# Four gathers underway with a full wait at group ends, and float32r products ahead of the bucket product

## What is computed

```python
h = (x @ W.T).reshape(n, 8, 64)
e = leaky_relu(e_src[src] + e_dst[dst], 0.2) * (1.0 + et_emb[edge_type]) * edge_weight[:, None]
e = jnp.exp(e - e_max[dst])
alpha = e / (e_sum[dst] + 1e-10)
msg = h[src] * alpha[:, :, None]
out = jnp.zeros((n, 8, 64), x.dtype).at[dst].add(msg).reshape(n, 512)
out = out + x          # then a layer norm with gamma and beta
```

## Time and profile before

| | us |
|---|---|
| median of 3 runs | 1774.82 |
| lowest and highest run | 1773.98, 1784.84 |
| the profiled execution | 1784.84 |
| its span, first to last instruction | 1783.1 |
| PE busy in it | 1662.2 (93%) |
| DVE busy | 883.9 (50%) |
| POOL busy | 652.3 (37%) |
| ACT busy | 500.9 (28%) |
| mean granted TensorE clock | 0.967 of 2.4 GHz |

### The profile page before, as it was taken

The page is one execution under the profiler, slowest core; times in us unless marked ns, Lnnn a source line. Parts: engine busy times, 40 slices in busy tenths (PEclk is TensorE's granted clock), DMA queues, the critical chain, the costliest instruction groups (busy, mean ns, idle before and its releaser), DMA issues.

```text
span 1783.1 us, 23533 instructions
## 1 busy us (share of the span) xinstructions
PE 1662.2 (93%) x7303; PEld 940.2 (53%) x7304; DVE 883.9 (50%) x2161; ACT 500.9 (28%) x1586; POOL 652.3 (37%) x756
## 2 busy tenths in 40 slices
PE   6989999999899999999999998797899999999998
PEld 4534444446655546455556766432444555555655
DVE  8878888888834443443443157785623101111322
ACT  1134444447422414133231225110200111111234
POOL 5868787873232323324342613666200000000000
PEclk9999999999999999999998997899899999999999
DMA  8031101005423123232216734356326121310020
GB/s 315 1 104 25 60 25 60 25 8 132 141 58 128 54 90 83 58 110 55 74 49 153 276 96 146 111 162 174 100 72 217 50 91 53 100 59 24 5 68 18
DMA packets 119614, 161.76 MB, mean 91 GB/s; under 512 B 49497, under 2 KB 61721, under 8 KB 119154
## 3 DMA queue, kind: packets, MB, share of 16 engines
q1 hardware_dynamic: 93056, 115.43, 21.0%
q0 software_dynamic: 18592, 29.91, 6.3%
q10 hardware_dynamic: 7890, 15.44, 2.7%
HBM read 145.26 MB, written 15.47 MB: 90 GB/s over the span
## 4 chain that ended last, share of the span: by engine, by line
PE 81%; DVE 9%; DMA 5%; issue 2%; ACT 2%; POOL 1%; ACTq 0%; DVEq 0%; POOLq 0%; SPq 0%
PE psum L373 79%; DMA ring<-tab_h,sd_t 2%; DMA arena<-tab_h,sd_t 1%; DVE stats L470 1%; DVE ring L1299 1%; DVE xn L2067 0%; PE psum L1028 0%; DVE xn L2073 0%; POOL ring L630 0%; DVE xn L2086 0%; ACT xT L414 0%; PE psum L2302 0%; DMA x<-in_x 0%; DVE ring L666 0%; DMA tab_h<-arena 0%
## 5 line engine op out<-in xcount | busy, mean ns | idle before, releaser
L373 PE MATMUL psum<-arena 128*128 128x384 f32 (+9 forms) x1804 | 315.3, 331 | 21.1 <-DVE arena L2688 8.0
L373 PE MATMUL psum<-arena,ring 128*128 (+1 forms) x1504 | 326.0, 363 | 9.5 <-issue 6.2
L373 PE MATMUL psum<-xT,ring 128*128 128x384 f32 x928 | 310.7, 495 | 6.8 <-ACT xT L414 4.2
L373 PE MATMUL psum<-ring,arena 128*128 128x512 f32 (+1 forms) x570 | 262.8, 604 | 15.3 <-DVE ring L666 10.5
L373 PEld LDWEIGHTS psum<-arena 128*128 128x128 f32 (+5 forms) x1804 | 195.1, 154 | 148.8 <-issue 74.7
L373 PE MATMUL psum<-ring,xT 128*128 128x512 f32 x552 | 251.1, 608 | 1.1 <-issue 0.7
L373 PEld LDWEIGHTS psum<-xT,ring 128*128 128x128 f32 x928 | 178.2, 193 | 133.2 <-issue 17.6
L373 PEld LDWEIGHTS psum<-arena,ring 128*128 128x128 bf16 (+1 forms) x1504 | 139.4, 115 | 131.3 <-issue 29.9
L373 PEld LDWEIGHTS psum<-ring,arena 128*128 128x128 f32 (+1 forms) x570 | 99.2, 187 | 140.4 <-issue 139.3
L1079 ACT ACTIVATE ring<-ring 128x128 f32<-128x128 f32 x416 | 123.3, 297 | 173.4 <-DVE ring L1365 161.4
L373 PEld LDWEIGHTS psum<-ring,xT 128*128 128x128 f32 x552 | 104.8, 195 | 124.1 <-issue 121.7
(11 more groups left out here) (478 smaller groups left out, 1737.0 us busy)
## 6 DMA issues: line engine op xcount, KB each, us to landing
ring<-in_L_ffn_w SPq DMA_DIRECT2D x22, 1024.0 KB, 7.3
ring<-in_L_gnn_m_w SPq DMA_DIRECT2D x8, 1024.0 KB, 6.1
ring<-in_L_ffn_expert_weights SPq DMA_DIRECT2D x8, 1024.0 KB, 5.5
ring<-tab_key ACTq DMA_DIRECT2D x24, 256.0 KB
ring<-in_L_gnn_Wv SPq DMA_DIRECT2D x5, 1024.0 KB, 5.0
tab_w<-xn SPq DMA_DIRECT2D x6, 768.0 KB, 15.3
ring<-in_L_gnn_Ww SPq DMA_DIRECT2D x4, 1024.0 KB, 18.6
ring<-in_L_gnn_wq SPq DMA_DIRECT2D x4, 1024.0 KB, 5.3
```

Of the source, the lines that this page charges most:

```text
L373: return nc.tensor.matmul(o, a, b, start=start, stop=stop)
```

## The change

In `pool_scatter_rows` the limit becomes four gathers underway, for every T. At each T above 0 that is a multiple of 6 (while T < 39) or of 12 (from 39 on), POOL waits for all earlier gathers to land before it issues the next: at T = 6, 12, 18, 24, 30, 36 and 48, 60, 72, 84, 96. The calls of `between` and the wait for `msg_used` stay where they are.

In the first layer PE's filler ahead of the bucket product changes from six `keep_clock` products to nine products of type float32r, of 512, 256 and 128 columns, three each, and three `keep_clock` products. Their operand is a new tile `zeros_r` in SBUF, which DVE fills with a copy of `zeros` as its first instruction.

```diff
--- before.py
+++ after.py
@@ -183,6 +183,7 @@
         x = sb("x", [P, NT, D])
         xn = sb("xn", [P, NT, D])
         xT = sb("xT", [P, KC, N])
+        zeros_r = sb("zeros_r", [P, 512], mybir.dt.float32r)
         xn2 = sb("xn2", [P, NT, D])
         xT2 = sb("xT2", [P, KC, N])
 
@@ -629,7 +630,8 @@
         def pool_gather(o, table, column, **more):
             return nc.gpsimd.indirect_dma_start(o, None, table, bass.IndirectOffsetOnAxis(ap=column.bitcast(U32), axis=0), **more)
 
-        UNDERWAY = (2, 3)
+        ROWS_UNDERWAY = 4
+        ROW_GROUP, LOOP_GROUP = 6, 12
 
         def row_landed(eng, T):
             earlier = 1 if T % UN < 2 * NT else 0
@@ -641,9 +643,11 @@
                 between(T)
                 if T >= GR:
                     pool.wait_ge(msg_used, T - GR + 1 + 2 * RB)
-                most = UNDERWAY[T >= GR]
-                if T >= most:
-                    row_landed(pool, T - most)
+                if T > 0 and T % (ROW_GROUP if T < GR else LOOP_GROUP) == 0:
+                    for k in range(max(T - ROWS_UNDERWAY, 0), T):
+                        row_landed(pool, k)
+                elif T >= ROWS_UNDERWAY:
+                    row_landed(pool, T - ROWS_UNDERWAY)
                 pool_gather(go_rows[T % GR], table, sd_t[:, T:T + 1]).then_inc(rows_landed[T % UN], 16)
 
         def dve_hot_rows(dve, i):
@@ -904,7 +908,9 @@
             for c in range(KC):
                 banks.drained(pe, f"l0x{c}")
             b = banks.open(pe, "bucket")
-            keep_clock(b, 6)
+            for w in (512, 512, 512, 256, 256, 256, 128, 128, 128):
+                mm(b[:, 0:w], zeros_r[:, 0:P], zeros_r[:, 0:w], True, True)
+            keep_clock(b, 3)
             pe.wait_ge(bucket_ready, 1)
             mm(b[:, 0:NBK], tri_b[:], total_b, True, True)
             mm(b[:, 16:16 + NBK], ones_b[:], total_b, True, True).then_inc(banks.full_of("bucket"), 1)
@@ -1189,6 +1195,7 @@
         def _(dve, od):
             V = nc.vector
             dve.wait_ge(consts_ready, 1)
+            V.tensor_copy(zeros_r[:], zeros[:])
             V.memset(ones_b[:], 1.0)
             V.memset(eps_col[:], EPS)
             V.tensor_copy(tri_b[:], tri[:])
```

## The result

The changed kernel takes 1786.46 us (7 runs, 1783.32 to 1793.24), the kernel before beside it 1776.73 us (7 runs). The ratio is 1.0056, with a 95% interval of 1.0038 to 1.0075: about 10 us slower, where 4 us faster was forecast. The sign was wrong, and 1786.46 lies outside the range of 1760 to 1783.

A forecast was written before the change was run, and what follows sets the result against it. It took POOL's gathers before the first multiply, then PE, then gather landings from 1200 us to bound the scatter. -6.0 (gathers) and +1.0 (filler) gave -5.0; without the stall -1.7; between them -4: 1771 us, range 1760 to 1783.

The forecast's parts named there:

- The reading of the kernel before: Third-layer scatter: POOL on the path before the multiplies; later, landings with three underway pace the loop, 1.49 us a gather.
- the stall at T=32: Scatter before T=39: one stall worth 7.0 us in the old profile; half of it was carried into the forecast.
- The early gathers, T=12 and T=19: Scatter start under the new rule: T=12 at 1104.9 in place of 1110.67, T=19 at 1120.0 us.
- No wait for POOL at L2701: DVE before the first multiply: its 5.26 us wait for POOL goes; first multiply at about 1139.4, not 1144.55.
- T=39: End of the early gathers: T=39 at 1157.6 us against 1169.75, 12.1 us ahead, with half the stall carried.
- The prediction's sum without the stall: Whole kernel if the runs lack the stall: -8.8 early gathers, +6.1 loop, +1.0 filler, -1.7 us.
- The loop: Gathers T=39 to 97: issue steps, five drains of 4.48 and hold-ups sum to 95.5 us against 89.34, 6.1 slower.
- The step that failed: Scatter at T=39: its buffer is free in time, since PE is done with tile 0 at about 1142 us.
- the slower rival: Loop drains at +14.7 and float32r at +3.2 outweigh 8.8 early gain: about +9, 1784 us; slower at all 0.3.
- The clock in the drains: Rival: PE idling in the loop's drains drops its clock, +3 us, 1774; chance 0.25, on top of others.
- The filler: Opening, ahead of the bucket product: float32r products at two cycles a column delay it, +1.0 us.

The follow-up runs named there:

- base_bounds: Kernel before plus only SP's run-time bounds check of a tile count, which all experiments carry; 1777.73 us, ratio 1.0005.
- filler_only: Kernel before with the bounds check, new float32r filler and its copy, old gather rule; 1775.50 us, ratio 0.9990.
- gathers_only_third: Second rerun of gathers_only unchanged, against the kernel before; 1778.07 us, ratio 1.0003.
- B: Group of kernels run together on one chip, sharing 21 runs of the kernel before at 1774.26 us.
- early_four: Kernel before with the bounds check and the new gather rule only for T below 20, old rule from T=20; 1771.79 us, ratio 0.9980.
- four_no_waits: Kernel before with the bounds check and four gathers underway throughout, no full waits; 1804.30 us, ratio 1.0165.
- A: Group of kernels run together on one chip, sharing 24 runs of the kernel before at 1777.43 us.
- D: Group of kernels run together on one chip, sharing 15 runs of the kernel before at 1775.85 us.
- half_rows_again: Rerun of half_rows unchanged, beside gathers_only_again, against the kernel before; ratio 1.0083.
- both_bounds: The whole change with the bounds check added, against the kernel before; 1789.62 us, ratio 1.0061.
- gathers_only: Changed kernel with the bounds check and the old filler, so only the new gather rule; against the kernel before 1790.52 us, ratio 1.0070.
- gathers_only_again: First rerun of gathers_only unchanged, against the kernel before; ratio 1.0077.
- three_early: Kernel before with the bounds check and three gathers underway instead of two up to T=19, no full waits; 1769.54 us, ratio 0.9953.
- half_rows: gathers_only with half a row fetched by each gather T=0 to 19 (wrong halves); against the kernel before 1775.35 us, ratio 0.9981.
- E: Group of kernels run together on one chip, sharing 15 runs of the kernel before at 1777.38 us.
- no_wait_48: gathers_only without its full wait at T=48; against the kernel before 1775.01 us, ratio 0.9996.
- C: Group of kernels run together on one chip, sharing 28 runs of the kernel before at 1778.07 us.

## Why the prediction went wrong, point by point

**The reading of the kernel before** held in its mechanisms: POOL on the path ahead of the first multiply, and the landing as the limit in the loop. What it left open, whether the other runs have the stall at T=32, decided much of the forecast. Its profile was longer than others in this very stage: T=0 to T=97 takes 178.4 us there, in base_bounds 172.9 and in filler_only 171.6.

**The early gathers, T=12 and T=19**: forecast 24.2 and 39.3 us after T=0, measured 23.2 and 39.9 in the profile of after. Right.

**"No wait for POOL at L2701"**: wrong in the profile of after. The prediction took it that the depth leaves DVE as it is. But the score phase was 6.5 us shorter (34.0 against 40.5), DVE came 5.0 us sooner (L2705 at 1115.05, 1120.07 before), and the wait stayed, 6.37 us. The first multiply came where forecast, 58.7 us after T=0 by both. POOL's end was forecast right, and the path now runs over it; that the prediction had its own end of DVE's work within 0.6 us of POOL's, so that the wrong path gave the same time, is luck.

**T=39**: forecast 76.9 us after T=0, measured 75.9 in after and 77.4 in gathers_only_third. The place was right. The gain was not, because the prediction took it from the earlier trace rows with its stall at T=32, 89.1 us, and carried half of the stall. A run without the stall has 82.1 to 83.4 (filler_only, base_bounds). So the gain is 4.7 to 7.5 us (82.1 or 83.4 less 75.9 or 77.4), and not 12.1. This is the term that was mis-sized. The prediction's sum without the stall had 8.8 for it and came to -1.7; so even that sum had it too large, and a value between the two sums carried the error into the forecast.

**The loop**: forecast 95.5 us (53 steps and five drains of 4.48), measured 96.3 in after and 96.2 in gathers_only_third; in after the steps onto the five full waits were 4.3 to 4.5 us, the others 1.40 on the mean. Right in size and in mechanism. Against base_bounds' 89.5 it is +6.8, and this alone cancels the early gain. That agrees with the 1.0003 of gathers_only_third. So even where nothing was held up, the 4 us forecast did not come.

**The step that failed** is the sentence that the buffer of T=39 is "free by then", and the assumption under it that the other engines work on the same beside four gathers as beside two. In three groups of five they did not. In B the first multiply came 69.0 and 94.9 us after T=0 in early_four and four_no_waits. In A and D it came 77.8 to 80.8 us after T=0 in place of 58.7, T=39 waited for its buffer 6 to 7 us, and a late start of the multiplies went together with the long gather behind the full wait at T=48 or T=60 (6.3 to 8.0 us; half_rows_again had none). The loop was then 99.5 to 103.2 us in place of 96.3. This makes the 12 to 16 us by which both_bounds, gathers_only, gathers_only_again and half_rows_again are slower than before. That the timed runs of the changed kernel, 10 us slower, had the same is an inference from both_bounds, since its own profile caught an execution without it. Why the engines are held up stays open. No rival had it; the slower rival named drains and a float32r price, and its sum of 1784 (the range ended at 1783) came near the measured time for another reason. That is luck.

**The clock in the drains**: a rival, and seen. The granted clock is 0.92 from 1210 to 1260 us in place of 1.00. Its price can't be separated from the drains' own, but the loop came out within 1 us of a sum that had no such term.

**The filler**: L1234 at 19.37 against 18.39, +0.98, as forecast. This is luck, for the time at which DVE takes the bucket product up differs by more than that between executions of the unchanged filler. In the 17 profiles that have it, it lies between 16.71 and 19.74 us: from 16.71 to 17.22 in eight, from 18.39 to 19.74 in nine. The three with the new filler have 19.30 to 19.59. The timeline of three_early, PE and then DVE, with the same twelve instructions that took 4.61 us in the earlier trace rows:

```profile
13.80 2.83 PE L373 MATMUL psum<-zeros 128*128 128x256 f32 x12 [0.67 <-ACT xT L414]
```

```profile
16.75 0.17 DVE L1227 TENSOR_SCALAR gate<-psum 128x9 f32<-128x9 f32 x1 [0.30 <-PE psum L373]
```

What differs is when PE's clock rises. In the kernel before these instructions follow each other every 0.427 us up to 17.25 and every 0.216 us from 17.5 on (so the prediction read its 17.05 well), in three_early at the short step from the start. The trace's first record of a granted clock, 1.00, starts at 17.32 in the one and at 13.36 in the other; ahead of it the column of the windows reads 1.00 for want of a record, and the steps tell the level. In the kernel after the record starts at 19.73, and the kept ones follow each other every 0.427 us to the end, which is 1.2 GHz, where the prediction priced them at 2.4 GHz. The nine float32r products take 2.59 us to the next instruction for 2688 columns, 0.96 ns a column, near one cycle a column at 1.2 GHz (0.83) and far from the two cycles chosen (1.67). So two errors of opposite sign met, on a basis that differs by 3 us from one execution to the next. In time it is nothing: filler_only 0.9990. (For this part the prediction has the numbers of two groups exchanged: the fillers stand in the earlier trace rows, the copy in the earlier trace rows.)

## What to carry to other kernels

Read a deeper queue and a full wait apart: here three and then four underway without full waits were worth 28 us, and four with full waits nothing or less. The gather onto a full wait came 4.3 to 4.5 us behind the one ahead of it in the kernel after, against 1.39 us a gather where nothing drained, so one full wait in twelve cost more than the fourth one underway brought. Before a gain is summed, take the stage's duration from more than one execution: part of the gain forecast here was a stall of 5.62 us that neither other profile of the old gather rule has. And where one kernel can gain on one occasion and lose on the next, run it again beside a rival before a cause is named, as half_rows shows.

## What the runs showed of the hardware that was not expected

- With four indirect gathers underway, PE, ACT and DVE, which take no gathered row in this phase, can be held up: in seven profiles DVE waited 12.4 to 24.6 us and ACT 11.6 to 19.9 of the 66 us from 1080 to 1146 for nothing that the trace names, and PE 8.5 to 23.2 us on issue (2.1 at most in the other profiles). The same kernel had it in all six timed runs of one group (1787.20 to 1795.33 us) and lacked it in all ten of another (1775.25 to 1781.47), if the times of the runs not profiled are read by those that were. Its cause stays open. The bytes of the early gathers are excluded (half_rows_again), and the chip by itself (groups B and E). One suspicion is the fetching of instructions. The Trainium skill (Runtime: NRT & Kernel Launch, "Instruction fetch mechanics") says that an engine's instructions come in 16 KiB blocks by a DMA queue of its own. Such blocks of 16384 bytes are in the traces: four of them start between 1091 and 1125 us in gathers_only and took 0.93 to 1.33 us each, and in no_wait_48 of group C five start between 1086 and 1112 and took 0.97 to 1.60. The transfers are no slower where the hold-up is, so these rows don't carry the suspicion, and it wasn't tested by a run.
- A gather behind a pause of POOL can take 5.6 to 8.0 us of issue in place of 0.95 when DVE multiplies back to back: T=32 of the kernel before, T=30, T=48 and T=60 in the runs above. All six such gathers ended with the same short DVE cast; T=48 of half_rows_again, in the same place, took 1.31 us.
- Three or four gathers underway without the hold-up went with a score phase of 33.9 to 34.7 us, two with 37.9 to 40.8.
- The rise of PE's clock in the opening moves the same twelve filler instructions from 4.61 us to 2.83 between executions of kernels that don't differ in this part.
- The copy of zeros into float32r takes 1.94 us on DVE (L1198), where a float32 copy of the same size took 0.42. That isn't shown to be the price of the type: in the kernel before, DVE's first two casts in the same place took 1.59 and 1.52 us for 128x128 elements, and 0.22 and 0.21 behind the copy in the kernel after. It runs beside the load of x and costs nothing that can be measured.
